# Attention to 257 keys: scores and maxima in smaller pieces, and the reads of the values' bank moved within a step

## The reference

```
h   = layernorm(x)                       # 128 x 32 x 128
q   = (h @ Wq + bq) * 8**-0.5            # 16 heads of 8 channels
k,v = ctx @ Wk + bk, ctx @ Wv            # 257 keys for each of the 128 sequences
s   = q . k, per head                    # 16 x 32 x 257 for each sequence
s   = s - 1e30 where the mask is 0       # t_cross alone
p   = softmax(s)                         # over 257 keys
x   = x + (p . v) @ Wo + bo
```

## Time and profile before

| | |
|---|---|
| median of 3 runs | 3989.83 us (3988.98 to 3995.96) |
| the profiled execution's own time | 3982.57 us |
| its span, first to last instruction | 3980.8 us |
| a_cross, first exponential to last | 20.2 to 505.2 us |
| e_cross | 2147.3 to 2632.8 us |
| t_cross | 2889.7 to 3375.9 us |
| granted TensorE clock in 100 to 500, 2200 to 2600 and 2900 to 3300 us | 1.00 of full speed |

### The profile page before, as it was taken

The page is one execution under the profiler, slowest core; times in us unless marked ns, Lnnn a source line. Parts: engine busy times, 40 slices in busy tenths (PEclk is TensorE's granted clock), DMA queues, the critical chain, the costliest instruction groups (busy, mean ns, idle before and its releaser), DMA issues. The chain is left out here.

```text
span 3980.8 us, 119953 instructions
## 1 busy us (share of the span) xinstructions
PE 3385.2 (85%) x44674; PEld 2469.3 (62%) x44674; DVE 2670.8 (67%) x7002; ACT 2362.3 (59%) x6308; POOL 2422.3 (61%) x2724
## 2 busy tenths in 40 slices
PE   7999959999999579698698999978499999786866
PEld 5777737777777467365466777745277777453444
DVE  6888757777777523477445888857778887754655
ACT  6777736666666334386124777745577777644633
POOL 6767656776777343574425887746367676845733
PEclk9999979999999689898799999989599999887968
DMA  2111110000000122101221111110011111000023
GB/s 75 36 42 36 36 70 6 8 11 11 8 6 2 63 72 77 47 14 47 67 72 59 51 45 42 37 60 4 17 37 36 42 36 30 3 2 6 2 93 94
DMA packets 90549, 149.05 MB, mean 37 GB/s; under 512 B 10112, under 2 KB 66816, under 8 KB 89664
## 3 DMA queue, kind: packets, MB, share of 16 engines
q1 hardware_dynamic: 79936, 122.87, 9.9%
q0 software_dynamic: 10240, 20.99, 1.7%
HBM read 112.76 MB, written 31.06 MB: 36 GB/s over the span
## 5 line engine op out<-in xcount | busy, mean ns | idle before, releaser
L2251 POOL TENSOR_TENSOR t_cross_E<-t_cross_E,t_cross_inverse 128x1028 f32<-128x1028 f32 x128 | 243.2, 1900 | 134.8 <-DVE t_cross_inverse L2530 134.8
L2251 POOL TENSOR_TENSOR a_cross_E<-a_cross_E,a_cross_inverse 128x1028 f32<-128x1028 f32 x128 | 243.2, 1900 | 132.8 <-DVE a_cross_inverse L2530 132.8
L2477 ACT ACTIVATE t_cross_E<-t_cross_psum,t_cross_negtop 128x257 f32<-128x257 f32 x512 | 238.8, 472 | 113.5 <-DVE t_cross_negtop L2520 110.0
L2477 ACT ACTIVATE a_cross_E<-a_cross_psum,a_cross_negtop 128x257 f32<-128x257 f32 x512 | 238.8, 472 | 112.4 <-DVE a_cross_negtop L2520 103.9
L2477 ACT ACTIVATE e_cross_E<-e_cross_psum,e_cross_negtop 128x257 f32<-128x257 f32 x512 | 238.8, 472 | 111.2 <-DVE e_cross_negtop L2520 103.3
L2251 POOL TENSOR_TENSOR e_cross_E<-e_cross_E,e_cross_inverse 128x1028 f32<-128x1028 f32 x128 | 243.2, 1900 | 94.2 <-DVE e_cross_inverse L2530 94.1
L3090 PEld LDWEIGHTS l_psum<-l_ffn_w,l_hidden 128*128 128x128 f32 x1536 | 197.9, 192 | 98.0 <-issue 56.1
L3090 PE MATMUL l_psum<-l_ffn_w,l_hidden 128*128 128x128 f32 x1536 | 207.8, 278 | 19.0 <-POOL l_hidden L2963 17.9
L3083 PE MATMUL l_psum<-l_hT,l_ffn_w 128*128 128x512 f32 x384 | 200.6, 625 | 0.9 <-ACT l_hT L3139 0.9
L2520 DVE TENSOR_REDUCE t_cross_negtop<-t_cross_psum 128x2 f32<-128x514 f32 x256 | 175.8, 687 | 32.6 <-PE t_cross_psum L2337 31.7
L2520 DVE TENSOR_REDUCE a_cross_negtop<-a_cross_psum 128x2 f32<-128x514 f32 x256 | 175.4, 686 | 26.8 <-PE a_cross_psum L2332 26.4
(11 more groups left out here) (754 smaller groups left out, 11124.1 us busy)
## 6 DMA issues: line engine op xcount, KB each, us to landing
a_cross_context<-context SPq DMA_DIRECT2D x32, 578.0 KB, 3.7
e_cross_context<-context SPq DMA_DIRECT2D x32, 578.0 KB, 3.7
t_cross_context<-context SPq DMA_DIRECT2D x32, 578.0 KB, 3.7
u_moe_weights<-pack_u_moe SPq DMA_DIRECT2D x1, 5633.0 KB, 16.3
slots<-l_blank SPq DMA_DIRECT2D x6, 832.0 KB, 12.2
a_moe_x_slots<-slots SPq DMA_DIRECT2D x26, 192.0 KB, 2.8
slots<-a_moe_y_slots SPq DMA_DIRECT2D x26, 192.0 KB, 2.1
c_moe_x_slots<-slots SPq DMA_DIRECT2D x26, 192.0 KB, 2.8
```

Of the source, the lines that this page charges most:

```text
L2251: pool.tensor_tensor(E[:, n % N], E[:, n % N], spread(inverse[:, n % 4], SK, 2), ALU.mult).then_inc(s_unit, 1)
L2477: act.activation(E[:, n % N, g], psum[:, g, 0:SK], ACT.Exp, bias=negtop[:, n % 2, g:g + 1], accum_out=total[:, n % 2, g:g + 1]).then_inc(s ...
```

## The change

PE: the scores are issued in two halves. Groups 0 and 1 wait only for exponentials 0 and 1 of the step before, groups 2 and 3 for all four; each half counts up `s_score`. In t_cross each half carries its two mask products. ACT: `second_half(n-3)` goes ahead of `values_out(n)`, and each exponential waits for its own maximum. DVE: four maxima of one group each instead of two of two groups. Behind the first two of them come, by phase, two of the four picks (3), `last_weights` and `output` (2), `last_values` (0), each of the three one step later in the program than before; then maximum 2, `keys(n+1)`, maximum 3, and in phase 3 the other two picks.

```diff
--- before.py
+++ after.py
@@ -2325,18 +2325,19 @@
                 pe.wait_ge(s_k, i * N + n + 1)
                 if n % 4 == 0:
                     pe.wait_ge(s_heads, i * 2 + n // 4 + 1)
-                if exists(i, n - 1):
-                    pe.wait_ge(s_exp, (i * N + n) * G)
-                for g in range(G):
-                    rows = slice(g * 32, (g + 1) * 32)
-                    last = pe.matmul(psum[:, g, 0:SK], q_heads[rows, n // 4 % 2, n % 4].rearrange("p j s -> p (j s)"),
-                                     kT[rows, n % 2], start=True, stop=mask is None)
-                if mask is not None:
-                    for g in range(G):
+                for half in range(2):
+                    if exists(i, n - 1):
+                        pe.wait_ge(s_exp, (i * N + n - 1) * G + 2 * half + 2)
+                    for g in (2 * half, 2 * half + 1):
                         rows = slice(g * 32, (g + 1) * 32)
-                        last = pe.matmul(psum[:, g, 0:SK], fold_bf[rows].rearrange("p j s -> p (j s)"), mask_neg[rows],
-                                         start=False, stop=True)
-                last.then_inc(s_score, 1)
+                        last = pe.matmul(psum[:, g, 0:SK], q_heads[rows, n // 4 % 2, n % 4].rearrange("p j s -> p (j s)"),
+                                         kT[rows, n % 2], start=True, stop=mask is None)
+                    if mask is not None:
+                        for g in (2 * half, 2 * half + 1):
+                            rows = slice(g * 32, (g + 1) * 32)
+                            last = pe.matmul(psum[:, g, 0:SK], fold_bf[rows].rearrange("p j s -> p (j s)"), mask_neg[rows],
+                                             start=False, stop=True)
+                    last.then_inc(s_score, 1)
 
             def side(i, n):
 
@@ -2472,17 +2473,16 @@
 
             def exponentials(i, n):
                 for g in range(G):
-                    if g % 2 == 0:
-                        act.wait_ge(s_top, (i * N + n) * 2 + g // 2 + 1)
+                    act.wait_ge(s_top, (i * N + n) * G + g + 1)
                     act.activation(E[:, n % N, g], psum[:, g, 0:SK], ACT.Exp, bias=negtop[:, n % 2, g:g + 1],
                                    accum_out=total[:, n % 2, g:g + 1]).then_inc(s_exp, 1)
 
             def step(i, n):
                 begin(i, n - 1)
+                if exists(i, n - 3):
+                    second_half(i, n - 3)
                 if exists(i, n):
                     values_out(i, n)
-                if exists(i, n - 3):
-                    second_half(i, n - 3)
                 side_out(i, n - 1)
                 if exists(i, n):
                     exponentials(i, n)
@@ -2513,10 +2513,10 @@
                 dve.tensor_copy(fold_bf[:], spread(core.const("fold"), J, 1)).then_inc(s_mask_ready, 1)
                 dve.tensor_scalar(mask_neg[:], mask_int[:], 0.0, -1e30, ALU.is_equal, ALU.mult).then_inc(s_mask_ready, 1)
 
-            def maximum(i, n, half):
-                if half == 0:
-                    dve.wait_ge(s_score, i * N + n + 1)
-                at = slice(2 * half, 2 * half + 2)
+            def maximum(i, n, g):
+                if g % 2 == 0:
+                    dve.wait_ge(s_score, (i * N + n) * 2 + g // 2 + 1)
+                at = slice(g, g + 1)
                 dve.tensor_reduce(negtop[:, n % 2, at], psum[:, at, 0:SK], AX.X, ALU.max, negate=True).then_inc(s_top, 1)
 
             def first_half(i, n):
@@ -2582,16 +2582,25 @@
                 picks = n % 4 == 3 and tile_exists(i, n // 4 - 1)
                 if exists(i, n - 1):
                     reciprocals(i, n - 1)
-                if picks:
-                    pick(i, n // 4 - 1, (0, 1, 2))
                 if exists(i, n):
                     maximum(i, n, 0)
+                    maximum(i, n, 1)
+                if picks:
+                    pick(i, n // 4 - 1, (0, 1))
+                if n % 4 == 2 and tile_exists(i, n // 4 - 1):
+                    last_weights(i, n // 4 - 1, n)
+                if n % 4 == 2 and tile_exists(i, n // 4 - 2):
+                    output(i, n // 4 - 2, n)
+                if n % 4 == 0 and tile_exists(i, n // 4 - 1):
+                    last_values(i, n // 4 - 1, n)
+                if exists(i, n):
+                    maximum(i, n, 2)
                 if exists(i, n + 1):
                     keys(i, n + 1)
                 if exists(i, n):
-                    maximum(i, n, 1)
+                    maximum(i, n, 3)
                 if picks:
-                    pick(i, n // 4 - 1, (3,))
+                    pick(i, n // 4 - 1, (2, 3))
                 if rest is not None and isinstance(i, int) and i == 0 and n == 0:
                     rest[1](dve)
                 if n % 4 == 0 and tile_exists(i, n // 4 + 2):
@@ -2601,12 +2610,6 @@
                 ahead = (i, n - 3) if n >= 3 else (i - 1, n + N - 3)
                 if fetch_of(*ahead) is not None:
                     add_result(fetch_of(*ahead))
-                if n % 4 == 1 and tile_exists(i, n // 4 - 1):
-                    last_weights(i, n // 4 - 1, n + 1)
-                if n % 4 == 1 and tile_exists(i, n // 4 - 2):
-                    output(i, n // 4 - 2, n + 1)
-                if n % 4 == 3 and tile_exists(i, n // 4):
-                    last_values(i, n // 4, n + 1)
 
             keys(0, 0)
             turns(dve, step, FETCHING + 1 if behind else 1)
```

## The result

The changed kernel takes 4141.16 us, the median of 4 runs (4138.67 to 4144.36), against 3989.40 for the kernel before (4 runs): a ratio of 1.0374, 95% interval 1.0358 to 1.0389. It is slower, as forecast, by 152 us where 77 were forecast, and 11 us above the top of the range. The profiled execution took 4144.36 us, with a span of 4142.6.

The account below looks back on a forecast made before the run. The prediction took the loop through maxima and exponentials as the bound, with PE having little slack. Four steps rise from 15.22 to 15.88 us (16.37 in t_cross), +77 us over three calls: 4067 us, range 3978 to 4130.

Parts of the forecast that it names:

- the exponentials' loop: Today's bound: ACT waits for maxima (41.2 us in 200), PE's scores for exponentials (16.3); claimed to go slack.
- the last piece of PE's tail: PE, from the values' sums until the next scores can start: taken as 0.42 us, between 0.37 and 0.57, of a 1.84 tail.
- Phase 3: 3.07 + 0.53 + 0.42: Phase 3 step of 4.02 us: next keys ready at 3.07, second turning 0.53, values' sums until next scores 0.42.
- The third rival: DVE's phase 3 operations end too late for the next first maximum, delaying phase 0: 4120 to 4173 us, chance 0.10.
- Take 0.90: PE, from the first half's start to the projected keys: 0.90 us, bounded by 0.68 and 1.05.
- The reads and maxima: DVE: maxima hold 0.35 us each, E_last and X take 0.30 and 0.29; PE waits 0.71 in phase 2, 0.41 in phase 0.
- Side work behind a wait: PE's side work up to the first turning: 0.33 us in phase 2, 0.22 in phase 0.
- 0.49 was predicted: t_cross's mask products: 0.08 us more in phases 0, 2 and 3, 0.25 in phase 1; four steps 16.37.
- PE never waits for the reads: Rival: DVE's reads done by S (first scores' start) + 1.41 us, leaving PE's own work: 3923 us, chance 0.15.
- The low ends hold: Rival: halves cost nearly nothing, maxima halve, gains and new waits cancel: no change, 3990 us, chance 0.10.
- DVE falls behind as well: The third rival: maxima of 0.40 or gaps at new waits use up DVE's phase 3 margin; 4120 to 4173 us, chance 0.10.
- all high ends would have to meet: Reason for little chance above 4130 us: keys at 1.05, maxima 0.40 and last piece 0.57 together give +183 us, 4173.

Follow-up runs that it names:

- r1: The changed kernel with last_weights, output and last_values put back at the end of the DVE step before: 4024.66 us, 1.0047 of the kernel before.
- r5: The kernel before with only the three bank reads moved behind its first (double) maximum: 4099.40 us, 1.0245 of the kernel before.
- r9: The changed kernel with the second pair of picks ahead of the fourth maximum instead of behind it: 4122.67 us, 1.0294 of the kernel before.
- r2: The changed kernel with the picks put back, three ahead of the maxima and one behind: 4099.86 us, 1.0239 of the kernel before.
- r12: The kernel before with only four single maxima, the keys ahead of the fourth, scores whole: 3961.92 us, 0.9892 of the kernel before.
- r4: The changed kernel with reads, picks and ACT's order all put back, leaving halves and single maxima: 3961.35 us, 0.9898 of the kernel before.
- r6: The kernel before with only the scores in halves, each double maximum waiting for its own half: 4008.78 us, 1.0012 of the kernel before.
- r10: Halves and single maxima on the kernel before, plus phase 3 reordered (three picks, maximum, keys, two maxima, pick, maximum): 3949.12 us, 0.9863.

## Why the prediction was wrong in size

The direction held, and so did the mechanism in phases 0 and 2: the exponentials' loop went slack, and a loop through the first half, two maxima, bank reads and PE's side work took its place (r1, r5). Two steps of the prediction failed: the last piece of PE's tail, and the path through phase 3, which goes on past the keys to the last pick. Four steps were to take 15.88 us and took 16.84. By the prediction's own steps, each read as a difference of means in a_cross:

- **"I take 0.42", the last piece of the tail: mis-sized.** From the values' sums to the next scores it is 0.57 in every step but the last of the loop's body (below), also where PE waits for nothing (206.31 to 206.88 and 210.71 to 211.28 after). The row of before, 208.33 to 208.90, had shown just this 0.57, and I took it to hold a wait. 0.15 a step, 0.60 in four: the largest term. Its upper end was in the range of the sum.
- **"Phase 3: 3.07 + 0.53 + 0.42": a wait was missed.** I followed the picks to the keys, and PE from the keys to its end as if it waited for nothing else. But `values` of the next tile, which goes into the bank that the picks read, waits for the last pick, and that stood behind the fourth maximum now. The values' sums start 1.07 behind the second turning, not 0.53: 0.54, of which 0.06 is what a turning behind a wait takes longer (0.59 to the values' sums in phase 2 of r1). r9 gives back 0.33 of it and r2 0.39; the rest of r2's 0.54 is the keys' earlier time. The third rival had those very DVE operations in its sum, and asked of them only whether the next maximum comes late.
- **"Take 0.90" for the keys: too high.** They start at S + 0.65, earlier than the lower bound of 0.68, and just as early behind undivided scores when ACT's copy is done (r12): the second pair costs nothing. In the phases where PE waits for DVE this changes nothing; in phase 1 it gives 0.25. The rule of the Trainium skill (TensorE: Matmul & The Clock Gate, The mechanism) that tiles of other row groups run side by side was right against my choice, and 0.65 lies below the 0.77 that I had worked out from it.
- **The reads and maxima: a little too long.** Held maxima are 0.34 (0.35 taken). E_last and X hold DVE 0.39 together (208.31 to 208.70), not 0.59: for X the sum took its duration, 0.29, where before it held DVE 0.21 on average until the next start. PE's side product starts at 2.01 in phase 2 (2.12 predicted), at 1.81 in phase 0 away from the loop's end (1.82), the turning of phase 3 at 2.93 (3.07): 0.27 less in all.
- **Side work behind a wait: a little too short.** In phase 2 from its start to the turning 0.41, not 0.33, and in phase 0 0.30, not 0.22: 0.15 more.
- **The end of the hardware loop.** Steps of phase 3 alternate between 4.57 and 4.75, those of phase 0 between 4.09 and 4.25, every other tile: the body of the loop holds two tiles. On average this gives 0.17 in four steps. The trace shows that it is PE's branch back: from the values' sums to the scores it is 0.74 to 0.79 us at each of the 13 places of a call where PE goes back to the loop's start, and 0.57 or 0.58 where the same two steps follow each other on the way into the loop and out of it, in all three calls. Behind the branch the second pair of scores starts 0.12 late as well, the eight take 0.82 and the keys start at S + 0.76. Why, stays open.

0.60 + 0.54 - 0.25 - 0.27 + 0.15 + 0.17 = 0.94, against 0.96 found. Times 32 and three calls that would be some 90 us over the forecast, and 75 were found: the first steps of each call have no reads and picks and are shorter than before, and a call is 6 us shorter than its 127 mean steps would be. The 13 us that the profiled executions differ by outside the calls' exponentials lie between the calls (1642.1 and 256.9 us before, 1648.9 and 263.7 after), almost all in code that no kernel here changes; over all thirteen kernels these stretches take 1642 to 1662 and 257 to 264, so I take the 13 for spread between executions. The medians differ by 152, and leave 4 for them.

t_cross: 17.26, 0.42 over a_cross, where 0.49 was predicted. The sum is near, its parts less so: the mask adds 0.10 or 0.11 in each phase, where 0.08 was put down for phases 0, 2 and 3 and 0.25 for phase 1.

**The rivals.** "PE never waits for the reads" fell, by the point it named: reads done at 1.41 or not, and they are done at 1.9. What it promised is there, though: in r12, which has the single maxima and leaves the reads where they were, phases 0 to 2 are 3.48, 3.62 and 3.50, PE's own work. The rule that I named beside it (the Trainium skill, Perfetto Trace Analysis, Optimizing Scalar/DVE Operations), that broken-up instructions may let work complete sooner, holds for that one part: 0.9892. "The low ends hold" had the keys' start right and nothing else. "DVE falls behind as well" gave a range that holds the result, 4120 to 4173, and not its reason: DVE idles ahead of every first maximum, 0.99 and 1.33 us above; what was late in phase 3 was PE, for a pick. The change's time is near the sum of all high ends by another way.

The range, 3978 to 4130, was too narrow above: I cut it there since "all high ends would have to meet", but the tail's high end was there in every step, and with the one unlisted wait it made 1.14, as much as all high ends together (1.10).

## What to carry to other kernels

When an operation is moved on one engine, list every semaphore that it raises, and follow each to all instructions behind it on the waiting engine, not only to the first one that asks; the wait that costs may be the second. When the waiting engine has little slack (PE's phases 0 to 2 took 3.70, 3.79 and 3.73 before, and 3.48, 3.62 and 3.50 in r12), an instruction that frees a buffer belongs in the idle time before the wait that starts the next round, not behind it: here the same three reads leave PE at its own work in one place (r4, r12) and cost 95 to 131 us in the other, while splitting the maxima, tried by itself, gave 1.1%. And a duration that a trace shows in one place only, with a wait beside it, goes into the sum as it stands until a row shows it shorter.

## What the runs showed of the hardware

- Eight records of the scores start in two rounds of four, 0.32 us apart, with 0.007 from one start to the next in a round. In two pairs of row groups each with a wait of its own they take 0.72 us together when no wait is open, as long as the undivided eight, and the 257-column product behind them starts at 0.65 in both (after, r12). A second pair that starts 0.18 late makes the eight 0.18 longer (r6, phase 1: 0.89), one that starts 0.25 late 0.25 (r10, phase 0: 0.97).
- A product group that starts behind a wait takes longer than the same behind others, by the start of the group behind it: from L2367's two records to the turning 0.41 (0.33 in the earlier trace rows), from the second turning to the values' sums 0.59 (r1, phase 2; 0.53 in the earlier trace rows). The undivided scores do not: 0.72 before, also behind their wait for the exponentials.
- Sixteen products of 128*32 tiles take 0.64, and products of 32*128 tiles behind them start 0.57 behind their start at the earliest, in all kernels here. Why no more of the last one is overlapped stays open.
- A branch back of the hardware loop makes PE's scores start 0.17 to 0.22 us later (13 times a call, none where the loop is entered or left).
- A maximum of 257 columns from PSUM takes 0.417 us on average and holds DVE 0.34 when another follows; one of 514 took 0.69 and held it 0.60. Two reads of 128 columns in a row, E_last and X, held it 0.20 each after; before, E_last held it 0.26 on average (0.30 in the earlier trace rows) and X 0.21.
